# A layer norm inside a transformer decoder: two averaging matmuls against turned token rows and VectorE's statistics

## The chip, the cores and the metric

One core of a Trainium2 chip. The metric is the device time of one execution in microseconds (us). Before the change three runs gave 2074.24, 2076.47 and 2077.68 us, median 2076.47.

## The reference

A gated linear attention layer, a cross attention and a six-layer local transformer stand in a row, each with a residual and a layer norm behind it. All is float32. The change lies in the six-layer part, which takes most of the time:

```python
for i in range(6):
    x = attn_layer(shift_tokens(x), Wqkv[i], q_scale[i], k_scale[i], Wo[i]) + x
    x = ffn_layer(shift_tokens(x), ln_g[i], ln_b[i], W1[i], b1[i], W2[i], b2[i]) + x

def ffn_layer(x, g, bln, W1, b1, W2, b2):
    mu = x.mean(-1, keepdims=True)
    var = ((x - mu) ** 2).mean(-1, keepdims=True)
    xn = (x - mu) / jnp.sqrt(var + 1e-05) * g + bln
    a, gate = jnp.split(xn @ W1 + b1, 2, -1)
    return a * jax.nn.gelu(gate, approximate=False) @ W2 + b2
```

`shift_tokens` moves the upper 64 of the 128 channels one token on. The attention has 16 heads of width 64, normed and rotated queries and keys, and windows of 32 queries that see 64 keys. There are 2048 rows of 128 channels in all, handled as 4 batches of 512.

## The kernel before

The state `x_all` lies in SBUF with channels on the partitions (128 x 2048). The six layers are one long pipeline of 96 blocks of 128 tokens (`ALL_BLOCKS`), `g` = 0 to 95, and three more turns to drain it. In one turn, `step(g)`, every engine works on several blocks at once: block `g` gets its queries and keys, block `g-1` its values and scores, block `g-2` its probabilities and weighted values, block `g-3` has its heads turned. `n = g % 4` is the place in the batch. In this text *step 0, 1, 2, 3* means a turn with that `n`. The feed-forward part of the batch that is two batches back, pass `f` (24 of them), is spread over the four steps: layer norm in step 0, the first six matmuls (`hid`, a gate and a value for each of three chunks) in step 1, the second ones (`ffn_project`) in steps 1 and 2. The output projection of the batch before, `project_out`, lies in steps 2 and 3.

The order is written out by hand, one `step` function for each engine, and each engine does its instructions in that order. Engines meet through semaphores. PSUM is four pairs of banks: `bank_x` (values, then scores), `bank_y` (turned heads, turned keys, key projection, weighted values), `bank_z` (queries, turned queries, turned probabilities) and `bank_f` (feed-forward). A `turn` is eight 128 x 128 transposes by TensorE against the identity.

TensorE's step: values' projection V (L697) in two halves with one signal at its end; turn the heads (L621, 8 transposes, each half once ScalarE has the heads copied); turn the keys (8) and the queries (8, L621), for which ScalarE must have copied the turned heads out of the same bank (L997); project the keys (L617 with WK), for which the turned keys must be copied out (L1009); half of the scores (L682); turn the probabilities (L621); the other half of the scores; half of the weighting (L689); project the next queries (L617 with WQ); the other half of the weighting. Between the turn of the heads and that of the keys something of the feed-forward part or the output projection stands in every step: in step 0 `centre` (L650), a matmul with I - 1/128 that takes the channel mean off; in step 1 `hid(1)`; in step 2 one chunk of `ffn_project` (L662); in step 3 three chunks of `project_out` (L643).

The layer norm in step 0 is: VectorE's `add_projected` (L1118, L1119 into `ffn_x`, L1124 into `x_all`, at the end of the step 3 before), TensorE's `centre`, ScalarE's `square` (L947), TensorE's `variance` (L655, a matmul with 1/128 that puts the mean square on all partitions), ScalarE's `inverse` (L951 Ln, L953 Exp), VectorE's `norm` (L1131 times scale and inverse deviation, L1133 plus bias). All these work on 128 x 512 elements, and for odd `f` the three of `add_projected` come in two pieces each.

VectorE's step: multiply the queries by cosine and sine (L1101, L1106), their square sums (`sums(0)`: L1146, L1150), the same products for the keys once ScalarE has squared them (L1029), the scores' maximum and subtraction (L1182, L1186), `norm`, the keys' square sums, the row sums of the probabilities. ScalarE's step: square the queries (L977), copy the heads (L959), copy the values (L989), copy the turned heads (L997), seed the mask (L1003), copy turned keys (L1009) and queries (L1014), invert the queries' norms (L965, L969), square the keys (L1029), copy the turned probabilities (L1034), exponentials (L1041). In step 1 a table load (L983) and the first `gelu` (L941) stand before the values' copy, and VectorE's `gated(f, 0)` (L1096) releases TensorE's second `hid`, L626.

## Time and profile before

| | |
|---|---|
| median of three runs | 2076.47 us |
| the profiled execution | 2077.16 us |
| its span | 2075.4 us |
| TensorE busy | 1973.1 us, 95% of the span |
| VectorE / ScalarE / GpSimd busy | 68% / 67% / 52% |
| the pipeline of steps | about 440 to 2045 us of the span |

The profiled execution is 1.76 us longer than its span, and 0.69 us longer than the median of the runs. In the chain that ended last TensorE has 88% of the span. A busy matmul is not a matmul at its peak: in a timeline the distance from one group's start to the next group's start is what the group takes in the queue, and the duration of a single instruction is longer, since instructions overlap. The text after calls that distance a pitch.

### The profile page before, as it was taken

How to read it: one execution, taken by the hardware profiler on the slowest of the kernel's cores; microseconds unless marked ns; L12 is line 12 of the kernel's file. 1: busy time of each engine (PE TensorE's matmuls, PEld its weight loads, DVE VectorE, ACT ScalarE, POOL GpSimd, SP SyncE). 2: the span in 40 equal slices, each digit the busy share in tenths (PEclk: the TensorE clock that was granted, in tenths of full speed). 3: DMA queues.
4: the chain of work that ended last, by engine and by line, in shares of the span. 5: the costliest groups of instructions: out<-in, count | busy, mean ns of one | idle time of the engine just before them, and what ended most of it. 6: DMA issues, size and time to landing. Idle time of an engine off the chain costs nothing.

```text
span 2075.4 us, 74512 instructions
## 1 busy us (share of the span) xinstructions
PE 1973.1 (95%) x32424; PEld 1171.9 (56%) x32424; DVE 1407.7 (68%) x1975; ACT 1393.9 (67%) x2125; POOL 1086.2 (52%) x709
## 2 busy tenths in 40 slices
PE   8989897789999999999999999999999999999997
PEld 5655654355555555555555655555555555555553
DVE  1454545677777777777777777777777787777762
ACT  5565564466777667776777677767776777677763
POOL 1000000496666666666666666666666666666650
PEclk9999998799999999999999999999999999999999
DMA  3000001132223222232222323222332223222220
GB/s 118 2 1 1 2 21 31 28 77 64 63 63 94 73 73 63 64 94 73 73 63 66 92 71 78 74 60 72 85 79 73 67 63 95 73 74 63 64 63 21
DMA packets 82210, 128.37 MB, mean 62 GB/s; under 512 B 17246, under 2 KB 28124, under 8 KB 81884
## 3 DMA queue, kind: packets, MB, share of 16 engines
q1 hardware_dynamic: 81884, 123.59, 22.9%
q8 instruction: 257, 4.21, 0.9%
q14 instruction: 69, 0.57, 0.1%
HBM read 21.81 MB, written 1.05 MB: 11 GB/s over the span
## 4 chain that ended last, share of the span: by engine, by line
PE 88%; ACT 5%; DVE 4%; issue 3%; DMA 0%; ACTq 0%; SPq 0%; DVEq 0%
PE ps L621 17%; PE ps L617 16%; PE ps L643 9%; PE ps L697 9%; PE ps L682 7%; PE ps L689 7%; PE ps L427 4%; PE ps L626 3%; PE ps L662 3%; PE ps L630 3%; DVE work L1254 2%; PE ps L523 2%; PE ps L441 1%; PE ps L655 1%; PE ps L650 1%
## 5 line engine op out<-in xcount | busy, mean ns | idle before, releaser
L1424 POOL TENSOR_TENSOR work<-work,RS 128x1024 f32<-128x1024 f32 x192 | 365.2, 1902 | 386.3 <-ACT RS L969 384.6
L1101 DVE TENSOR_TENSOR work<-ps,work 128x512 f32<-128x512 f32 (+1 forms) x288 | 247.7, 860 | 328.9 <-ACT work L1029 292.3
L621 PEld LDWEIGHTS ps<-ident,work 128*128 128x128 f32 x3072 | 342.8, 141 | 141.3 <-issue 104.7
L621 PE MATMUL ps<-ident,work 128*128 128x128 f32 x3072 | 394.2, 275 | 6.3 <-ACT work L997 2.4
L1443 POOL TENSOR_TENSOR work<-work 128x1024 f32<-128x1024 f32 x96 | 225.9, 2354 | 99.0 <-DVE work L1106 99.0
L1435 POOL TENSOR_TENSOR work<-work 128x1024 f32<-128x1024 f32 x96 | 227.2, 2367 | 69.1 <-DVE work L1106 69.1
L1106 DVE TENSOR_TENSOR work<-ps,work 128x512 f32<-128x512 f32 (+1 forms) x288 | 247.2, 858 | 0.0
L1041 ACT ACTIVATE work<-work 128x1024 f32<-128x1024 f32 x96 | 101.5, 1057 | 205.1 <-DVE work L1186 204.7
L1146 DVE TENSOR_REDUCE SS<-work 128x16 f32<-128x1024 f32 x192 | 232.0, 1208 | 0.0
L689 PEld LDWEIGHTS ps<-work 64*32 64x32 f32 x12288 | 134.8, 105 | 147.7 <-issue 132.9
L617 PE MATMUL ps<-WQ,XS 128*128 128x512 f32 x384 | 189.3, 616 | 8.0 <-issue 4.4
L682 PEld LDWEIGHTS ps<-KT,work 64*32 64x32 f32 x12288 | 135.8, 105 | 105.5 <-issue 105.5
L643 PE MATMUL ps<-work,WO 128*128 128x512 f32 x384 | 193.5, 617 | 1.2 <-issue 1.2
L697 PE MATMUL ps<-WV,XS 128*128 128x512 f32 x384 | 190.9, 620 | 1.7 <-DVE work L1186 1.7
L1430 POOL TENSOR_TENSOR work<-work,RL 128x1024 f32<-128x1024 f32 x96 | 183.1, 1907 | 10.6 <-DVE RL L1197 10.6
L617 PE MATMUL ps<-WK,XS 128*128 128x512 f32 x384 | 185.0, 604 | 0.1
L682 PE MATMUL ps<-KT,work 64*32 64x64 f32 x12288 | 169.1, 224 | 15.0 <-issue 15.0
L689 PE MATMUL ps<-work 64*32 64x64 f32 x12288 | 167.6, 224 | 4.2 <-issue 3.0
L1034 ACT ACTIVATE work<-ps 128x1024 f32<-128x1024 f32 x96 | 98.3, 1024 | 85.1 <-PE ps L621 85.1
L1456 POOL TENSOR_TENSOR work<-work 128x512 f32<-128x512 f32 x16 | 16.5, 1040 | 258.5 <-PE ps L461 136.6
L989 ACT ACTIVATE work<-ps 128x1024 f32<-128x1024 f32 x96 | 98.6, 1027 | 51.1 <-PE ps L697 51.1
L1182 DVE TENSOR_REDUCE MX<-ps 128x16 f32<-128x1024 f32 x96 | 116.9, 1218 | 19.4 <-PE ps L682 19.4
(184 smaller groups left out, 3091.8 us busy)
## 6 DMA issues: line engine op xcount, KB each, us to landing
work<-work SPq DMA_DIRECT2D x576, 128.0 KB
work<-work SPq DMA_DIRECT2D x336, 64.0 KB
WQ<-in_wqkv SPq DMA_DIRECT2D x6, 512.0 KB, 3.6
WK<-in_wqkv SPq DMA_DIRECT2D x6, 512.0 KB, 4.5
WV<-in_wqkv SPq DMA_DIRECT2D x6, 512.0 KB, 3.5
WO<-in_wo SPq DMA_DIRECT2D x6, 512.0 KB, 3.8
work<-ZR SPq DMA_DIRECT2D x48, 64.0 KB
W<-in_w SPq DMA_DIRECT2D x6, 341.0 KB, 3.2
```

What stands on the lines that cost most here:

```text
L617: return mm(R[:, half, :], x_shift[:, 32 + at * 128:160 + at * 128], w[:, half * 512:half * 512 + 512], start=True, stop=True)
L621: m = nc.tensor.transpose(flat(R)[:, t * 128:t * 128 + 128], src[:, t * 128:t * 128 + 128], ident[:, :])
L643: m = mm(bank_f[:, 0, :], w_o[:, k, :], heads_t[:, k, 128 * (f % 2):128 * (f % 2) + 512], start=k == 0, stop=k == 7)
L682: m = mm(bank_x[32 * w:32 * w + 32, q, c8 * 64:c8 * 64 + 64], q_t[64 * q:64 * q + 64, c8, 32 * w:32 * w + 32], k_t[64 * q:64 * q + 64, c8, ...
L689: m = mm(bank_y[32 * w:32 * w + 32, q, c8 * 64:c8 * 64 + 64], probs_t[64 * q:64 * q + 64, c8, 32 * w:32 * w + 32], v_win[64 * q:64 * q + 6 ...
L697: m = mm(bank_x[:, q, :].rearrange('p (c d) -> p c d', d=64), x_shift[:, 32 + nb * 128:160 + nb * 128], w_v[:, :].rearrange('p (c q d) -> ...
L1101: V.tensor_tensor(h16(cos_part[:, j, cols]), h16(src), rotary_tabs[:, at:at + 64].unsqueeze(1).broadcast_to([PARTS, heads_in, 64]), ALU.mu ...
L1106: V.tensor_tensor(halves(sin_part[:, j, cols]), halves(src)[:, :, ::-1, :], rotary_tabs[:, at:at + 64].rearrange('p (s d) -> p s d', d=32) ...
L1146: V.tensor_reduce(sq_sums[:, j, :, 0], h16(squares[:, j, :]), AX, ALU.add).then_inc(done, 1)
L1424: U.tensor_tensor(h16(qk_norm[:, j, :]), h16(cos_part[:, j, :]), inv_norms[:, j, :].unsqueeze(2).broadcast_to([PARTS, 16, 64]), ALU.mult). ...
L1435: U.tensor_tensor(cos_part[:, 0, :], cos_part[:, 0, :], sin_part[:, 0, :], ALU.add).then_inc(q_rotated, 1)
L1443: U.tensor_tensor(cos_part[:, 1, :], cos_part[:, 1, :], sin_part[:, 1, :], ALU.add).then_inc(k_rotated, 1)
```

## The change

Four things are changed.

1. `centre` becomes `turn_tokens`: four transposes of `ffn_x` into `bank_f`, so that tokens lie on the partitions. It stands right behind V, ahead of the turn of the heads. `variance` becomes `turn_back`, four transposes of the normed rows, at the place of `variance`.
2. Mean and variance of a token are now taken by VectorE's row statistics (`moments`: four `bn_stats`, four `bn_aggr`), the inverse deviation by ScalarE on 128 x 4 elements instead of 128 x 512, and `norm` is four `tensor_scalar` of 128 x 128 with the mean and the inverse deviation of the row. ScalarE's `square` is gone, and `inverse` stands in its place, ahead of the queries' norms. Scale and bias are applied after the turn back by one instruction (`affine`) at the place of the old `norm`.
3. `add_projected` is cut in two. The addition into `x_all` (`add_to_x`) moves from the end of step 3 into step 0, behind the queries' sine product. `moments` follows it, then the queries' square sums, then `norm`.
4. In every step the two halves of V signal apart (`values_ready` counts twice), and ScalarE copies them in two instructions of 512 columns instead of one of 1024. Who waits for these semaphores waits for twice the count.

In the last pass, outside the steps, the same functions stand in the same order, with the last norm's instructions among them.

```diff
     ffn_x = sb('YS', [PARTS, SEQ])
-    centred = sb('YC', [PARTS, SEQ])
-    spread = sb('YQ', [PARTS, SEQ])
-    normed = sb('YR', [PARTS, SEQ])
+    centred = sb('YC', [PARTS, 4, PARTS])
+    ffn_stats = sb('YT', [PARTS, 4, 6])
+    ffn_moment = sb('YM', [PARTS, 4, 2])
+    ffn_rstd = sb('YQ', [PARTS, 4])
...
-            def centre(f):
+            def turn_tokens(f):
                 pe.wait_ge(ffn_shifted, f + 1)
                 pe.wait_ge(x_updated, f + 4)
-                mm(bank_f[:, 1, :], centre_w[:, :], ffn_x[:, :], start=True, stop=True).then_inc(ffn_centred, 1)
-
-            def variance(f):
-                pe.wait_ge(ffn_squared, f + 1)
+                for j in range(4):
+                    m = nc.tensor.transpose(bank_f[:, 1, j * 128:j * 128 + 128], ffn_x[:, j * 128:j * 128 + 128], ident[:, :])
+                m.then_inc(ffn_turned, 1)
+
+            def turn_back(f):
+                pe.wait_ge(ffn_centred, f + 1)
                 pe.wait_ge(x_plus_attn, f + 1)
-                mm(bank_f[:, 0, :], mean_w[:, :], spread[:, :], start=True, stop=True).then_inc(ffn_variance, 1)
+                for j in range(4):
+                    m = nc.tensor.transpose(bank_f[:, 0, j * 128:j * 128 + 128], centred[:, j, :], ident[:, :])
+                m.then_inc(ffn_returned, 1)
...
                     for q in range(2):
-                        m = mm(bank_x[:, q, :].rearrange('p (c d) -> p c d', d=64), x_shift[:, 32 + nb * 128:160 + nb * 128], w_v[:, :].rearrange('p (c q d) -> p q c d', q=2, d=64)[:, q], start=True, stop=True)
-                    m.then_inc(values_ready, 1)
+                        mm(bank_x[:, q, :].rearrange('p (c d) -> p c d', d=64), x_shift[:, 32 + nb * 128:160 + nb * 128], w_v[:, :].rearrange('p (c q d) -> p q c d', q=2, d=64)[:, q], start=True, stop=True).then_inc(values_ready, 1)
...
+                if f is not None and n == 0:
+                    turn_tokens(f)
                 if d:
                     pe.wait_ge(heads_copied, g - 2)
                     turn(bank_y, heads, 0, 4).then_inc(heads_turned, 1)
                     turn(bank_y, heads, 4, 8).then_inc(heads_turned, 1)
-                if f is not None and n == 0:
-                    centre(f)
...
-            def square(f):
-                act.wait_ge(ffn_centred, f + 1)
+            def inverse(f):
+                act.wait_ge(ffn_moments, f + 1)
                 if due(f):
-                    act.wait_ge(ffn_normed, f)
-                A(spread[:, :], bank_f[:, 1, :], ACT.Square).then_inc(ffn_squared, 1)
-
-            def inverse(f):
-                act.wait_ge(ffn_variance, f + 1)
-                A(spread[:, :], bank_f[:, 0, :], ACT.Ln, bias=tiny[:, 0:1]).then_inc(ffn_log, 1)
+                    act.wait_ge(ffn_centred, f)
+                A(ffn_rstd[:, :], ffn_moment[:, :, 1], ACT.Ln, bias=tiny[:, 0:1]).then_inc(ffn_log, 1)
                 act.wait_ge(ffn_log, f + 1)
-                A(spread[:, :], spread[:, :], ACT.Exp, scale=-0.5).then_inc(ffn_inverse, 1)
+                A(ffn_rstd[:, :], ffn_rstd[:, :], ACT.Exp, scale=-0.5).then_inc(ffn_inverse, 1)
...
                 if b:
-                    act.wait_ge(values_ready, g)
-                    if due(g - 1):
-                        act.wait_ge(windows_loaded, 160 * (g - 1))
-                    A(v_rows[:, (n - 1) % 2, :], flat(bank_x), ACT.Copy).then_inc(values_copied, 1)
+                    for q in range(2):
+                        act.wait_ge(values_ready, 2 * g - 1 + q)
+                        if due(g - 1):
+                            act.wait_ge(windows_loaded, 160 * (g - 1))
+                        A(v_rows[:, (n - 1) % 2, 512 * q:512 * q + 512], bank_x[:, q, :], ACT.Copy).then_inc(values_copied, 1)
...
+            def add_to_x(f):
                 dve.wait_ge(ffn_shifted, f + 1)
...
+            def moments(f):
+                dve.wait_ge(ffn_turned, f + 1)
+                if due(f):
+                    dve.wait_ge(ffn_moments, f)
+                for j in range(4):
+                    m = V.bn_stats(ffn_stats[:, j, :], bank_f[:, 1, j * 128:j * 128 + 128])
+                m.then_inc(ffn_sampled, 1)
+                dve.wait_ge(ffn_sampled, f + 1)
+                if due(f):
+                    dve.wait_ge(ffn_centred, f)
+                for j in range(4):
+                    m = V.bn_aggr(ffn_moment[:, j, :], ffn_stats[:, j, :])
+                m.then_inc(ffn_moments, 1)
+
             def norm(f):
                 dve.wait_ge(ffn_inverse, f + 1)
                 if due(f):
+                    dve.wait_ge(ffn_returned, f)
+                for j in range(4):
+                    m = V.tensor_scalar(centred[:, j, :], bank_f[:, 1, j * 128:j * 128 + 128], ffn_moment[:, j, 0:1], ffn_rstd[:, j:j + 1], ALU.subtract, ALU.mult)
+                m.then_inc(ffn_centred, 1)
+
+            def affine(f):
+                dve.wait_ge(ffn_returned, f + 1)
+                if due(f):
                     dve.wait_ge(hidden_ready, 3 * f)
-                V.scalar_tensor_tensor(out=bank_f[:, 0, :], in0=bank_f[:, 1, :], scalar=layer_vecs[:, f // 4 * 9 + 6:f // 4 * 9 + 7], in1=spread[:, :], op0=ALU.mult, op1=ALU.mult).then_inc(ffn_normed, 1)
-                dve.wait_ge(ffn_normed, f + 1)
-                V.tensor_scalar(ffn_in[:, :], bank_f[:, 0, :], layer_vecs[:, f // 4 * 9 + 7:f // 4 * 9 + 8], None, ALU.add).then_inc(ffn_input, 1)
+                V.tensor_scalar(ffn_in[:, :], bank_f[:, 0, :], layer_vecs[:, f // 4 * 9 + 6:f // 4 * 9 + 7], layer_vecs[:, f // 4 * 9 + 7:f // 4 * 9 + 8], ALU.mult, ALU.add).then_inc(ffn_input, 1)
...
+                if f is not None and n == 0:
+                    add_to_x(f)
+                    moments(f)
+                if a:
                     sums(0, g)
+                if f is not None and n == 0:
+                    norm(f)
...
                 if f is not None and n == 0:
-                    norm(f)
+                    affine(f)
```

TensorE's row at step 0 before, from V to the next V (L697 is V, L650 `centre`, L655 `variance`):

```order
647 L697 MATMUL ps<-WV,XS 128x512 x2
648 L621 MATMUL ps<-ident,work 128x128 x8
649 L650 MATMUL ps<-YS,centre_w 128x512
650 L621 MATMUL ps<-ident,work 128x128 x16
651 L617 MATMUL ps<-WK,XS 128x512 x2
652 L682 MATMUL ps<-KT,work 32x64 x32
653 L621 MATMUL ps<-ident,work 128x128 x8
654 L682 MATMUL ps<-KT,work 32x64 x32
655 L655 MATMUL ps<-YQ,mean_w 128x512
656 L689 MATMUL ps<-work 32x64 x32
```

The same place now (L704 is V, L654 `turn_tokens`, L623 the turns, L661 `turn_back`):

```order
640 L704 MATMUL ps<-WV,XS 128x512 x2
641 L654 MATMUL ps<-ident,YS 128x128 x4
642 L623 MATMUL ps<-ident,work 128x128 x24
643 L619 MATMUL ps<-WK,XS 128x512 x2
644 L689 MATMUL ps<-KT,work 32x64 x32
645 L623 MATMUL ps<-ident,work 128x128 x8
646 L689 MATMUL ps<-KT,work 32x64 x32
647 L661 MATMUL ps<-ident,YC 128x128 x4
648 L696 MATMUL ps<-work 32x64 x32
```

Nothing stands between the turn of the heads and that of the keys any more.

VectorE's row before, from the shifted addition at the end of step 3 to the first products of the keys in step 0:

```order
903 L1118 TENSOR_TENSOR YS<-ps,X 64x128
904 L1119 TENSOR_TENSOR YS<-ps,X 64x128
905 L1118 TENSOR_TENSOR YS<-ps,X 64x384
906 L1119 TENSOR_TENSOR YS<-ps,X 64x383
907 L1124 TENSOR_TENSOR X<-ps,X 128x128
908 L1124 TENSOR_TENSOR X<-ps,X 128x384
909 L1101 TENSOR_TENSOR work<-ps,work 128x1024
910 L1106 TENSOR_TENSOR work<-ps,work 128x1024
911 L1146 TENSOR_REDUCE SS<-work 128x16
912 L1150 TENSOR_REDUCE SL<-SS 128x16
913 L1101 TENSOR_TENSOR work<-ps,work 128x512
```

The same place now, for an even `f`, where the additions are in one piece (L1170 and L1174 are the square sums, L1128 the addition into `x_all`):

```order
991 L1119 TENSOR_TENSOR YS<-ps,X 64x512
992 L1120 TENSOR_TENSOR YS<-ps,X 64x511
993 L1101 TENSOR_TENSOR work<-ps,work 128x1024
994 L1106 TENSOR_TENSOR work<-ps,work 128x1024
995 L1128 TENSOR_TENSOR X<-ps,X 128x512
996 L1136 BN_STATS YT<-ps 128x6 x4
997 L1142 BN_AGGR YM<-YT 128x2 x4
998 L1170 TENSOR_REDUCE SS<-work 128x16
999 L1174 TENSOR_REDUCE SL<-SS 128x16
1000 L1150 TENSOR_SCALAR YC<-ps,YM,YQ 128x128 x4
1001 L1101 TENSOR_TENSOR work<-ps,work 128x512
```

Twelve instructions now stand between the queries' sine product and the keys' cosine product that were not there, and the addition into `x_all` has come down past the two products of the queries.

## Rows read from the trace of the kernel before

**Rows 1.** Page's chain; a stretch: us, PE, PEld, DVE, ACT, POOL busy, clock, DMA.

```profile
PE 88%; ACT 5%; DVE 4%; issue 3%; DMA 0%; ACTq 0%; SPq 0%; DVEq 0%
...
450.00:2050.00 1600.00, 1576.41 (x28774) 928.02 (x28774) 1177.49 (x1535) 1136.99 (x1782) 1009.16 (x642) 1.00 0.28 71
```

**Rows 2.** Timeline of PE, one step 0 and into step 1: start, us, line.

```profile
845.88 1.98 PE L697 MATMUL ps<-WV,XS 128*128 128x512 f32 x4
847.70 1.04 PE L621 MATMUL ps<-ident,work 128*128 128x128 f32 x8
848.57 1.02 PE L650 MATMUL ps<-YS,centre_w 128*128 128x512 f32 x2
849.56 2.05 PE L621 MATMUL ps<-ident,work 128*128 128x128 f32 x16
851.48 1.95 PE L617 MATMUL ps<-WK,XS 128*128 128x512 f32 x4
...
855.97 1.12 PE L655 MATMUL ps<-YQ,mean_w 128*128 128x512 f32 x2
857.03 0.86 PE L689 MATMUL ps<-work 64*32 64x64 f32 x64
...
865.12 1.12 PE L626 MATMUL ps<-YN,W 128*128 128x512 f32 x2
```

**Rows 3.** Timeline of ACT, the same step.

```profile
847.90 1.03 ACT L989 ACTIVATE work<-ps 128x1024 f32<-128x1024 f32 x1 [0.77 <-PE ps L697]
848.82 1.08 ACT L997 ACTIVATE work<-ps 128x512 f32<-128x512 f32 x2
...
850.72 1.10 ACT L1009 ACTIVATE KT<-ps 128x512 f32<-128x512 f32 x2
851.67 1.06 ACT L1014 ACTIVATE work<-ps 128x1024 f32<-128x1024 f32 x1
...
853.05 0.27 ACT L965 ACTIVATE LS<-SL 128x16 f32<-128x16 f32 x1
...
853.48 1.07 ACT L1029 ACTIVATE work<-ps 128x512 f32<-128x512 f32 x2
```

**Rows 4.** Timeline of DVE, the same step.

```profile
846.85 0.56 DVE L1119 TENSOR_TENSOR YS<-ps,X 64x383 f32<-64x383 f32 x1
847.45 0.76 DVE L1124 TENSOR_TENSOR X<-ps,X 128x128 f32<-128x128 f32 x2
848.12 1.22 DVE L1101 TENSOR_TENSOR work<-ps,work 128x1024 f32<-128x1024 f32 x1
...
850.38 1.21 DVE L1146 TENSOR_REDUCE SS<-work 128x16 f32<-128x1024 f32 x1
...
854.09 0.69 DVE L1101 TENSOR_TENSOR work<-ps,work 128x512 f32<-128x512 f32 x1 [2.28 <-ACT work L1029]
854.70 0.68 DVE L1106 TENSOR_TENSOR work<-ps,work 128x512 f32<-128x512 f32 x1
```

**Rows 5.** Timeline of PE, a step 2: the turns of keys and queries.

```profile
880.23 1.98 PE L697 MATMUL ps<-WV,XS 128*128 128x512 f32 x4
...
883.90 1.94 PE L621 MATMUL ps<-ident,work 128*128 128x128 f32 x16
885.83 1.95 PE L617 MATMUL ps<-WK,XS 128*128 128x512 f32 x4
```

**Rows 6.** Timeline of DVE early in the span: prices of small instructions.

```profile
52.99 1.64 DVE L1268 BATCH_NORM_STATS2 work<-work 128x6 f32<-128x128 f32 x8
...
94.62 0.80 DVE L1279 TENSOR_SCALAR work<-ps,work 128x512 f32<-128x512 f32 x1
95.34 1.11 DVE L1284 BATCH_NORM_AGGREGATE work<-work 128x2 f32<-128x24 f32 x8
```

**Rows 7.** Waits of the whole span, and PE at the last pass.

```profile
PE ps L682 <- issue: 15.0, 17, 1.5
...
2055.01 1.13 PE L626 MATMUL ps<-YN,W 128*128 128x512 f32 x2 [3.02 <-DVE YN L1133]
```

More of the change, by code:

```diff
@@ L307, in decoder @@
     gates_ready = nc.alloc_semaphore('gates_ready')
+    ffn_turned = nc.alloc_semaphore('ffn_turned')
+    ffn_sampled = nc.alloc_semaphore('ffn_sampled')
+    ffn_moments = nc.alloc_semaphore('ffn_moments')
+    ffn_returned = nc.alloc_semaphore('ffn_returned')
     HIDDEN_CHUNKS = [128, 128, 85]
@@ L361, in windows @@
                 before = v_rows[:, (m + 1) % 2, :]
-                sp.wait_ge(values_copied, m + 1)
+                sp.wait_ge(values_copied, 2 * (m + 1))
                 for q in range(2):
@@ L382, in _ @@
                         sp.dma_start(w_k[:, :], io['wqkv'][l + 1, :, 1024:2048]).then_inc(wk_loaded, 16)
-                        sp.wait_ge(values_ready, l * 16 + 16)
+                        sp.wait_ge(values_ready, 2 * (l * 16 + 16))
                         sp.dma_start(w_v[:, :], io['wqkv'][l + 1, :, 2048:3072]).then_inc(wv_loaded, 16)
@@ L752, in step @@
                 if f is not None and n == 0:
-                    variance(f)
+                    turn_back(f)
                 if f is not None and n == 1:
@@ L790, in finish @@
                 last_centre(2)
-                centre(f)
+                turn_tokens(f)
                 last_variance(2)
-                variance(f)
+                turn_back(f)
                 pe.wait_ge(ffn_input, f + 1)
@@ L1000, in step @@
                 if b:
-                    act.wait_ge(values_copied, g)
+                    act.wait_ge(values_copied, 2 * g)
                     seed = window_mask[:, 0 if n == 1 else 1, :]
@@ L1019, in step @@
                 if f is not None and n == 0:
-                    square(f)
+                    inverse(f)
                 if f is not None and n == 1:
@@ L1034, in step @@
                     A(probs_t[:, :, :], turned(bank_z), ACT.Copy).then_inc(probs_turned_copied, 1)
-                if f is not None and n == 0:
-                    inverse(f)
                 if b:
@@ L1061, in finish @@
                 last_inverse(1)
-                square(f)
                 last_square(2)
@@ L1106, in rotary_sin @@
                 V.tensor_tensor(halves(sin_part[:, j, cols]), halves(src)[:, :, ::-1, :], rotary_tabs[:, at:at + 64].rearrange('p (s d) -> p s d', d=32).unsqueeze(1).broadcast_to([PARTS, heads_in, 2, 32]), ALU.mult).then_inc(done, 1)
+            places = lambda f: ((0, 128, 384), (128, 512, 0)) if f % 2 else ((0, 512, 0),)
             def add_projected(f):
@@ L1112, in add_projected @@
                 if due(f):
-                    dve.wait_ge(ffn_centred, f)
+                    dve.wait_ge(ffn_turned, f)
                 xo = f % 4 * 512
-                parts = ((0, 128, 384), (128, 512, 0)) if f % 2 else ((0, 512, 0),)
-                for first, last, at in parts:
+                for first, last, at in places(f):
                     end = min(last, 511)
@@ L1120, in add_projected @@
                 m.then_inc(ffn_shifted, 1)
+            def add_to_x(f):
                 dve.wait_ge(ffn_shifted, f + 1)
-                for first, last, at in parts:
+                xo = f % 4 * 512
+                for first, last, at in places(f):
                     xc = x_all[:, xo + first:xo + last]
@@ L1216, in finish @@
                 add_projected(f)
+                add_to_x(f)
+                moments(f)
                 last_scale(0)
@@ L1219, in finish @@
                 norm(f)
+                affine(f)
                 last_scale(2)
@@ L1406, in stage @@
                 if due(g - 3):
-                    pool.wait_ge(values_ready, g - 3)
+                    pool.wait_ge(values_ready, 2 * (g - 3))
                 pool.wait_ge(x_updated, bt + 1)
```

3 lines of the change are left out of this document (removed).

## The prediction

> **What bounds the kernel.** I read the page's chain of waits first: TensorE (PE) has 88% of it. The table of stretches then shows it busy for 1576 of the 1600 us from 450 to 2050, at a granted clock of 1.00, its 2.4 GHz level [rows 1]. So only what shortens PE's row, or lets it wait less inside what looks busy, can help. Then I read the timelines of the three engines in one step 0 side by side, all times below counted from the start of V (845.88) [rows 2 to 4].
>
> PE: heads turned from 1.82 (the start of its row less 845.88, and so on), `centre` from 2.69, keys' and queries' turns (16) from 3.68, key projection from 5.60, `variance` from 10.09 for 1.06, weighting from 11.15. Eight transposes take 0.87 (1.82 to 2.69), so four cost 0.43. The sixteen take 1.92, against 1.74 at that pitch: PE looks busy there but is held. By what? ScalarE's row answers: values' copy at 2.02, turned heads' copies at 2.94, just as that ends, first half done some 0.60 later at 3.53, and PE goes at 3.68. Turned keys' copies begin at 4.84, the first half is done at 5.45, and the key projection starts at 5.60. Both gaps are 0.15, the usual delay from a ScalarE copy to a matmul here. So up to 5.60 step 0 is set by ScalarE, and `centre` filled a hole. Step 2 is the same to the hundredth: sixteen turns at 3.67, key projection at 5.60 [rows 5].
>
> The other thread runs from the keys' products on VectorE. They start at 8.21 (854.09), wait for ScalarE's square at 7.60, and release in turn the maximum, subtraction, exponential, two copies, two small inverses, the table load, `gelu`, `gated` and PE's second `hid` at 19.24 (865.12) [rows 2 to 4]: 11.03 later. PE by itself reaches that `hid` at the same moment: the weighting, the next queries and the weighting's second half take it from 11.15 to the next V at 14.64, then come 1.82 of V, two matmuls at 0.86, 0.2 to signal and 0.8 of `gated`, 4.6 in all: 19.24. Two threads end together, so the later one will decide.
>
> **Part by part.**
>
> *PE's matmuls.* Per pass `centre` (0.99) becomes four transposes (0.43), and `variance` (1.06 behind scores, 0.19 of it the switch from small tiles) becomes 0.43 plus a switch of about 0.15, an estimate, 0.58. Naively 1.04 x 24 = 25 us less PE work. The question is how much of it is on the path.
>
> *Values in halves.* The first half is complete 0.91 earlier. ScalarE was idle for 0.77 before the values' copy, so from 1.25 [rows 3]. It now copies half 0 until about 1.76 and half 1 from 2.02 to 2.50, at 0.48 each (two of 512 columns in 0.95, as the turned heads' copies show when the mask follows). In step 2 the first turned heads' half is ready at 2.50 too. Its copy is done at 3.10, so the keys' turns need not wait: 1.82 + 0.87 + 0.86 for the chunk of `ffn_project` = 3.55. Sixteen turns at 1.74 give 5.29. The turned keys' copy: heads' copies to 3.45, mask 0.95 to 4.40, first half done 5.01, PE may go at 5.16, so 5.29 stands. The key projection, 1.88 when late, takes 1.81 when it isn't. In sum 0.31 + 0.07, call it 0.37 a step. The keys' squares come 0.30 earlier as well, so VectorE follows. 22 passes: -8.1 us. Bounds: 0, if ScalarE is late anyway, and -0.45 a step, the whole time that it is free sooner, which is -9.9 us. In steps 1 and 3 more matmuls stand as a cover, and nothing comes of it. In the first layer's steps there is no cover at all and dependencies set the pace. I take -1 there (0 to -1.8, four times 0.45).
>
> *Step 0 up to the key projection.* `turn_tokens` takes 1.82 to 2.26 (its input is ready at 1.53 [rows 4]), heads' turn 2.26 to 3.13. ScalarE is free at 2.50 but the first turned half comes only at 2.91. Its copy ends at 3.50, PE's keys' turns at 3.65, before 3.68. ScalarE's row then runs 0.03 ahead of before and the key projection starts at 5.57. `centre`'s saving is gone: the wait takes its place, and the split pays only for that.
>
> *VectorE in step 0.* The addition moves down by two products: no change in sum, but the products come 0.7 earlier and the queries' turn, which needed the sine product, is free of it. Added: four `bn_stats`, (1.64 - 0.28) / 7 = 0.195 each; four `bn_aggr`, (1.11 - 0.20) / 7 = 0.13 each on 24 numbers, here 6, I take 0.12; four `tensor_scalar` with two scalars. That form took 0.72 pitch on 512 columns [rows 6]; less 384 columns at 1.04 ns, which the 1024 against the 512 column products show (1.13 against 0.60 [rows 4]), it is 0.32. Unpipelined each would be at most 0.28, 0.20 and 0.41. The row for an odd `f` (additions in two pieces): products from 1.56 to 3.82, addition to 4.49, `bn_stats` to 5.27, 0.1 for the result, `bn_aggr` to 5.91, queries' sums to 7.26, `norm` 1.28 to 8.54. For an even `f` the row is 0.34 earlier, but `norm` then waits for ScalarE: turned queries' copy from 5.74, 0.90, then Ln and Exp at 0.25 each, ready at 7.17, `norm` to 8.45. The keys' squares lie at 7.75 or before and are not last. So the keys' products begin at 8.54 or 8.45 in place of 8.21: 0.33 or 0.24 late. `square` held ScalarE for 0.48 (L1014 to L965 is 1.38, of which 0.90 the copy) and Ln and Exp now take as much at its place; Ln and Exp of 512 behind `variance` are gone, but there ScalarE was waiting.
>
> *The rest of step 0 and into step 1.* `turn_back` saves 0.48, but the weighting needs the keys' last product: 8.54 + 2.48 + 0.06 = 11.08, against 11.15. The second `hid` follows the products at 11.03: 19.57 or 19.48, against 19.24. `affine` (0.67) for two instructions gives VectorE 0.7 back behind the subtraction, and the keys' sums come earlier, yet ScalarE's queue behind the exponential is what the thread passes through. So a pass without a stall of PE loses 0.24 to 0.33. PE's own issue of instructions stalls in the scores now and then (17 waits, 0.9 each on average, in all kinds of steps [rows 7]). Where that comes in the second scores of a step 0, VectorE catches up, only PE's thread counts and 0.4 is saved. I read the second `hid`'s distance from V in the 22 passes one by one, 19.24 to 20.58: 8 undisturbed (19.24 to 19.30), together +2.0; 8 with PE 0.1 to 0.4 late, +0.0; 6 with PE over 0.7 late, -2.5. Sum -0.5. Bounds: with `norm` at a cost of nothing the undisturbed ones lose nothing and the late ones gain 0.25, -4.6 in all; with all twelve small instructions unpipelined (1.12 + 0.80 + 1.64 = 3.6 against 2.55), 1.0 more, +17.
>
> *Last pass.* Its norm lies open: PE waits 3.02 for the last norm row before its first `hid` [rows 7]. There 0.99 and 1.06 of matmul, the square and the Ln and Exp of 512 columns (each about 0.6, as the copies of that size) go out of a series, 3.9 in sum; 0.43 and 0.43 of transposes, 1.4 of statistics, 0.5 of Ln and Exp and 1.28 of `norm` for 0.7 come in, 3.3. With two matmul latencies less exposed to others' queues I take -1.0 (-2 to +1).
>
> Sum: -8.1 - 1 - 0.5 - 1 = -10.6 on the profiled 2077.16, 2066.6. The median of the runs is 0.69 lower; I give 2066.5.
>
> *A rule against it.* Small VectorE instructions here cost no more than their columns and about 0.06 [rows 6], but the `bn_stats` row reads SBUF, and the kernel now reads PSUM. The Trainium skill ("Perfetto Trace Analysis", Optimizing Scalar/DVE Operations) puts the access overhead of a VectorE instruction at about 60 ns for SBUF and about 125 ns for PSUM. By that the eight PSUM readers cost 0.5 more a pass, an estimate by that page, and the sum would be near 2076; rows 4 have PSUM reads of 1024 and 512 columns at 1.13 and 0.60, which leaves 0.07 for the fixed part, so I go by these. That result is my first rival.
>
> **Rivals.**
>
> 1. *VectorE's small instructions cost about 0.5 a pass more than I take.* For: no row has `bn_stats` from PSUM, nor a wait between such groups. Against: products from PSUM show a fixed part of 0.07. Price: undisturbed and late passes 16 x 0.5, nothing in the others, +8: 2075, no change.
>
> 2. *The keys' products are pushed beyond what the split gives back: slower.* Place: VectorE's row in step 0, ahead of the keys' products. It decides once they start 0.8 later than before (8.21), since then 16 x 0.8 outweighs the 10 of the other terms. At full unpipelined price it is 1.3 later, and the sum +17 - 10 = +7: 2084. For: two dependent waits, 12 short instructions. Against: rows 6 are pipelined.
>
> 3. *The split gives nothing in step 2*, since ScalarE is held by its heads' copy or a second wait costs as much: -2.5 in all, 2074. Against: it is idle 0.77 before the values' copy [rows 3].
>
> 4. *PE's stalls by issue come elsewhere or grow* when PE runs closer to its instruction fetch; 15 us in 17 waits could move by 4 either way [rows 7]. 2070 with a loss.
>
> 5. *VectorE is quick and its thread has slack.* Step 0 loses nothing: 2062; with `turn_back`'s whole 0.48 in every pass, 2055.
>
> 6. *More transposes lower the clock.* PE makes 32 transposes in every step, and the granted clock of the stretch is 1.00 [rows 1]; eight more in each fourth step should not matter. If a tenth of the 1600 us went at half the clock, 160 us would be added: 2230. The Trainium skill ("TensorE: Matmul & The Clock Gate", Part 4: PE-mode transpose) says that transposes do not count as PE being busy in the same way; the trace gives that rule no hold here.
>
> **Chances.** Forecast 0.48 (2061 to 2071); rival 1 0.15; 2 0.11; 3 and 4 0.13; 5 0.12; 6 0.01. A measurement of this kernel tells about 0.2%, 4.2 us, from no change. Faster takes the forecast, rival 5 and a part of 4 and 1: 0.69. Same 0.19, slower 0.12. The range 2058 to 2079 leaves out the lower half of rival 5 and most of 2; the likeliest case alone is 2061 to 2071.
>
> **What would show it.** Step 2 from V to the key projection 7.1 less 1.81, so 5.3 for 5.60. Step 0: key projection still at 5.57, PE or its loads held by the turned heads' copy in front of the keys' turns; weighting at 11.1; second `hid` at 19.5 where undisturbed. `bn_stats` at 0.2, `norm` four at 0.32. VectorE's keys' products waiting for nothing in odd passes. I am wrong if the key projection of step 2 still starts 5.6 behind V, or if the keys' products start beyond 8.7.

## The result, and the profile after

The changed kernel takes 2070.55 us (median of 11 runs, 2066.19 to 2074.26); the kernel before took 2077.48 in the runs beside it. The ratio is 0.9969 [0.996, 0.9977]: faster by 6.9 us. 2066.5 was predicted. The profiled execution took 2071.80 with a span of 2070.0, against 2077.16 and 2075.4: 5.4 less.

From the page: the engines' busy time, the queue that carries instructions, the shares of the chain. Then the stretch of [rows 1], with the same columns (length, busy time of PE, PEld, DVE, ACT and POOL, granted clock, DMA).

```profile
PE 1947.8 (94%) x32520; PEld 1179.6 (57%) x32520; DVE 1449.9 (70%) x2239; ACT 1371.7 (66%) x2197; POOL 1087.3 (53%) x709
...
q8 instruction: 257, 4.21, 0.9%
...
PE 73%; ACT 10%; DVE 10%; issue 6%; DMA 0%; ACTq 0%; SPq 0%; DVEq 0%
```

```profile
450.00:2050.00 1600.00, 1553.68 (x28881) 936.86 (x28878) 1222.23 (x1803) 1118.28 (x1856) 1010.84 (x642) 1.00 0.28 72
```

PE's busy time in this stretch fell by 22.7 us, just about what the prediction called naive, and its idle time rose from 23.6 to 46.3 by the same row of before [rows 1]. So PE now waits for nearly all that it saves. The chain says for whom: PE's share went from 88% to 73%, ScalarE's from 5% to 10%, VectorE's from 4% to 10%, issue from 3% to 6%. The clock stayed at 1.00.

Where the 5.4 us of the profiled executions are, measured from the start of V in one step to the start of V in the next, in us:

| part | before | after | difference |
|---|---|---|---|
| up to the first V | 396.06 | 396.91 | +0.9 |
| the first layer's seven steps | 108.04 | 107.09 | -0.95 |
| the 22 steps 0 | 330.8 | 329.2 | -1.5 |
| the 22 steps 1 | 433.5 | 436.4 | +3.0 |
| the 22 steps 2 | 364.5 | 357.9 | -6.6 |
| the 22 steps 3 | 373.5 | 373.5 | 0.0 |
| behind the last V | 69.1 | 69.0 | -0.1 |

The first line is chance: no edit touches that part, and in the other eleven traces it ends anywhere from 392.5 to 398.3.

In this text a time without a unit is in us, and a start within a step counts from the start of its V. One step 0, PE, the columns of [rows 2]; V starts at 845.52:

```profile
845.52 1.98 PE L704 MATMUL ps<-WV,XS 128*128 128x512 f32 x4
847.34 0.60 PE L654 MATMUL ps<-ident,YS 128*128 128x128 f32 x4
847.78 1.04 PE L623 MATMUL ps<-ident,work 128*128 128x128 f32 x8
849.22 1.94 PE L623 MATMUL ps<-ident,work 128*128 128x128 f32 x16 [0.40 <-ACT work L1000]
851.14 1.96 PE L619 MATMUL ps<-WK,XS 128*128 128x512 f32 x4
...
855.62 0.66 PE L661 MATMUL ps<-ident,YC 128*128 128x128 f32 x4
856.67 1.16 PE L696 MATMUL ps<-work 64*32 64x64 f32 x64 [0.39 <-DVE work L1106]
...
865.11 1.12 PE L628 MATMUL ps<-YN,W 128*128 128x512 f32 x2
```

The token rows are turned in 0.44 where `centre` took 0.99 [rows 2]. PE then stands for 0.40 in front of the keys' turns, until ScalarE's copy of the turned heads is through, and the key projection starts at 5.62; before 5.60. The way back (L661) is short too, and behind it PE waits 0.39 for a product of VectorE: the weighting starts at 11.15, as before. The second `hid` is at 19.59, before 19.24. These two waits now recur in nearly every pass. PE's waits, 450 to 2000 (us in total, times, longest), of the kernel after and then of before:

```profile
PE ps L689 <- issue: 10.6, 14, 1.3
PE ps L623 <- ACT work L1000: 10.0, 24, 0.7
PE ps L696 <- DVE work L1106: 6.9, 18, 0.4
PE ps L696 <- issue: 3.7, 8, 1.1
```

```profile
PE ps L682 <- issue: 12.6, 15, 1.5
...
PE ps L621 <- ACT work L997: 1.2, 2, 0.8
...
PE ps L689 <- DVE work L1106: 0.4, 1, 0.4
```

Two waits of 1.6 us in total became 16.9. VectorE and ScalarE in the same step 0, as in [rows 4] and [rows 3]:

```profile
850.02 0.88 DVE L1136 BATCH_NORM_STATS2 YT<-ps 128x6 f32<-128x128 f32 x4
850.93 0.38 DVE L1142 BATCH_NORM_AGGREGATE YM<-YT 128x2 f32<-128x6 f32 x4
...
852.45 0.19 DVE L1174 TENSOR_REDUCE SL<-SS 128x16 f32<-128x32 f32 x1
852.86 1.37 DVE L1150 TENSOR_SCALAR YC<-ps,YM,YQ 128x128 f32<-128x128 f32 x4 [0.22 <-ACT YQ L955]
854.14 0.68 DVE L1101 TENSOR_TENSOR work<-ps,work 128x512 f32<-128x512 f32 x1
```

```profile
846.68 0.60 ACT L992 ACTIVATE work<-ps 128x512 f32<-128x512 f32 x1
847.54 0.60 ACT L992 ACTIVATE work<-ps 128x512 f32<-128x512 f32 x1 [0.26 <-PE ps L704]
848.48 1.09 ACT L1000 ACTIVATE work<-ps 128x512 f32<-128x512 f32 x2 [0.33 <-PE ps L623]
...
851.35 1.05 ACT L1017 ACTIVATE work<-ps 128x1024 f32<-128x1024 f32 x1
852.25 0.33 ACT L953 ACTIVATE YQ<-YM,tiny 128x4 f32<-128x4 f32 x1
852.61 0.21 ACT L955 ACTIVATE YQ<-YQ 128x4 f32<-128x4 f32 x1
```

VectorE is done with the queries' sums at 7.12 and waits 0.22 for ScalarE's Exp (L955), which ends at 7.30. `norm` starts at 7.34 and the keys' products at 8.62; before 8.21. This is a pass of odd `f`, with the addition in two pieces (L1128 x2). Such a pass is called heavier below, since VectorE's row is longer in it, and one of even `f` lighter. Even in the heavier one ScalarE ends last. In 21 of the 22 passes the products start at 8.62 (8.91 in the other).

Step 2, PE, against [rows 5]: the sixteen turns take 1.75 instead of 1.93 and the key projection starts 5.30 behind V, not 5.60.

```profile
880.21 1.98 PE L704 MATMUL ps<-WV,XS 128*128 128x512 f32 x4
...
883.76 1.91 PE L623 MATMUL ps<-ident,work 128*128 128x128 f32 x16
885.51 1.02 PE L619 MATMUL ps<-WK,XS 128*128 128x512 f32 x2
```

The last pass, against [rows 7]:

```profile
2048.08 2.08 PE L628 MATMUL ps<-YN,W 128*128 128x512 f32 x2 [0.90 <-DVE YN L1157]
```

This `hid` is 6.93 earlier in the span than before, while the projection ahead of the norm (L645, before L643) ends 5.81 earlier: the open norm is shorter by 1.1. But here the first pair of matmuls took 2.08 where it took 1.13 [rows 7]. The granted clock says why. A stretch of the kernel after, then two of the kernel before, with the columns of [rows 1]:

```profile
2046.90:2053.70 6.80, 5.89 (x9) 2.52 (x8) 2.16 (x3) 1.30 (x3) 0.00 (x0) 0.50 0.11 39
```

```profile
2055.00:2056.10 1.10, 1.09 (x3) 0.62 (x4) 0.55 (x1) 0.91 (x1) 0.00 (x0) 1.00 0.07 15
2056.30:2059.60 3.30, 3.30 (x5) 1.33 (x4) 0.75 (x1) 0.79 (x2) 0.00 (x0) 0.50 0.23 82
```

After, TensorE's granted clock fell to 0.50, its 1.2 GHz level, at about 2046.9 and stayed there until 2053.7, and the first three pairs of `hid` lie in that stretch. PE had waited 1.01 and 1.71 in the norm just before. Before, it fell only at 2056.2, behind the first pair, and until 2059.6. A matmul of 512 columns has a pitch of 0.85 there instead of 0.43. The six pairs of this `hid` take 1.09 longer than before, which gives the 1.1 back.

### The profile page after: what moved, and what is told of

Its sections match the earlier page's. It is cut to its first block, busy times and chain, and to the rows that moved or that the text cites. A ratio compares the mean times of both kernels' runs of the same rounds, so it can differ in the third digit from the quotient of the medians.

```text
span 2070.0 us, 75204 instructions
## 1 busy us (share of the span) xinstructions
PE 1947.8 (94%) x32520; PEld 1179.6 (57%) x32520; DVE 1449.9 (70%) x2239; ACT 1371.7 (66%) x2197; POOL 1087.3 (53%) x709
## 4 chain that ended last, share of the span: by engine, by line
PE 73%; ACT 10%; DVE 10%; issue 6%; DMA 0%; ACTq 0%; SPq 0%; DVEq 0%
PE ps L619 13%; PE ps L623 13%; PE ps L645 9%; PE ps L704 7%; PE ps L696 6%; PE ps L689 6%; PE ps L429 4%; PE ps L669 3%; PE ps L628 3%; PE ps L632 2%; DVE work L1287 2%; DVE work L1106 2%; PE ps L525 2%; PE ps L443 1%; ACT work L1000 1%
## 5 line engine op out<-in xcount | busy, mean ns | idle before, releaser
L623 PEld LDWEIGHTS ps<-ident,work 128*128 128x128 f32 x3072 | 344.1, 141 | 118.6 <-issue 90.0
L623 PE MATMUL ps<-ident,work 128*128 128x128 f32 x3072 | 392.8, 275 | 14.6 <-ACT work L1000 11.2
L1170 DVE TENSOR_REDUCE SS<-work 128x16 f32<-128x1024 f32 x192 | 231.6, 1206 | 0.0
L645 PE MATMUL ps<-work,WO 128*128 128x512 f32 x384 | 193.4, 618 | 0.0
L704 PE MATMUL ps<-WV,XS 128*128 128x512 f32 x384 | 191.0, 620 | 1.8 <-DVE work L1216 1.8
L689 PE MATMUL ps<-KT,work 64*32 64x64 f32 x12288 | 168.6, 224 | 13.3 <-issue 13.3
L1037 ACT ACTIVATE work<-ps 128x1024 f32<-128x1024 f32 x96 | 98.5, 1026 | 84.8 <-PE ps L623 84.8
L1012 ACT ACTIVATE KT<-ps 128x512 f32<-128x512 f32 x192 | 104.1, 600 | 31.8 <-PE ps L623 31.8
```

The lines of the kernel that those rows point to most:

```text
L623: m = nc.tensor.transpose(flat(R)[:, t * 128:t * 128 + 128], src[:, t * 128:t * 128 + 128], ident[:, :])
L645: m = mm(bank_f[:, 0, :], w_o[:, k, :], heads_t[:, k, 128 * (f % 2):128 * (f % 2) + 512], start=k == 0, stop=k == 7)
L689: m = mm(bank_x[32 * w:32 * w + 32, q, c8 * 64:c8 * 64 + 64], q_t[64 * q:64 * q + 64, c8, 32 * w:32 * w + 32], k_t[64 * q:64 * q + 64, c8, ...
L704: mm(bank_x[:, q, :].rearrange('p (c d) -> p c d', d=64), x_shift[:, 32 + nb * 128:160 + nb * 128], w_v[:, :].rearrange('p (c q d) -> p q ...
L1170: V.tensor_reduce(sq_sums[:, j, :, 0], h16(squares[:, j, :]), AX, ALU.add).then_inc(done, 1)
```

## The experiments

Medians are of the runs of each kernel, ratios (with 95% intervals) against the kernel before, run beside it. Differences between two of the changed kernels are taken from their ratios, times 2077 us. Starts and sums of steps are from one profiled execution of each.

### Each half of the change alone

*Halves only*: the kernel before, with values' projection signalled and copied in halves.

```
-   m = mm(bank_x[:, q, :]...)          # two, then m.then_inc(values_ready, 1)
+   mm(bank_x[:, q, :]...).then_inc(values_ready, 1)
-   A(v_rows[:, (n - 1) % 2, :], flat(bank_x), ACT.Copy)
+   for q in range(2):
+       act.wait_ge(values_ready, 2 * g - 1 + q)
+       A(v_rows[:, (n - 1) % 2, 512 * q:512 * q + 512], bank_x[:, q, :], ACT.Copy)
```

> The kernel before with the values' projection signalled and copied in halves, the layer norm left as it was. Theory A (the copy in halves is what gains, the norm by token rows costs): the keys' projection in step 2 starts 0.37 earlier as in the changed kernel (-8), the first layer about -1, and step 0, which still has the centring matmul as a cover, gains 0.3 to 0.37 too, since ScalarE's copies and with them VectorE's products of the keys come 0.3 earlier (-7): about -16 in all, 2061, faster than the changed kernel. Rival B (the two matmuls saved on TensorE are what gains): no more than -2, about 2075. Rival C (both add up, the norm is worth nothing either way): -7, like the changed kernel, 2070.

Measured: 2060.11 us, 0.9931 [0.9917, 0.9944], near the 2061 of theory A.

*Norm only*: the changed kernel with these edits taken back.

> The changed kernel with one signal and one copy for the values, as before; the layer norm by token rows stays. Theory A: step 2 at 5.60 from the values' projection to that of the keys again, step 0 the same 5.60, VectorE's products of the keys in step 0 0.3 late, the second hidden matmul 0.2 to 0.35 late where TensorE does not stall: 0 to +5, 2077 to 2082. Rival B (less work on TensorE gains): -10 or more, 2067 or less.

Measured: 2076.93, 1.0012 [1.0002, 1.0022]: 2.5 us slower than before, and no 10 us faster as rival B had it. Its keys' products start at 8.61, its step 2 stays at 16.35. One step 0 of *halves only*, VectorE; V at 842.71:

```profile
850.85 0.69 DVE L1101 TENSOR_TENSOR work<-ps,work 128x512 f32<-128x512 f32 x1 [2.22 <-ACT work L1029]
```

The keys' products start at 8.14 there (7.88 in the lighter passes), 0.5 to 0.7 before those of the changed kernel, and the second `hid` at 19.19 (median) instead of 19.60. So the halves alone bring twice what the whole change brings, and the norm by token rows takes about half of it away: 0.0038 of 2077 is 7.9 us, of which the passes show 5.3 in the steps 0 (323.9 against 329.2), 2.2 in the steps 1, 1.1 in the steps 2.

### Where the token rows' turns stand

*Token rows behind the heads*: in the changed kernel the four transposes go behind the heads' turns.

```
-   if f is not None and n == 0: turn_tokens(f)
    (the turns of both heads)
+   if f is not None and n == 0: turn_tokens(f)
```

> The changed kernel with the four transposes of the feed-forward input behind the turn of the heads, where the centring matmul stood, and not ahead of it. Theory A (VectorE's row in step 0 sets the weighting and the second hidden matmul): the projection of the keys in step 0 starts at about 5.2 in place of 5.6, but the weighting still at 11.1 and the hidden matmul where it was: no more than -1 us against the changed kernel, about 2070. Rival D (the lost cover of the keys' turns is what holds step 0): 22 times 0.4, -9, 2062.

Measured: 2058.15, 0.9928 [0.9912, 0.9943], 8.5 less than the changed kernel by the ratios. Theory A is wrong, and rival D, the lost cover, came out. (A cover is work that PE does while ScalarE copies what PE needs next.) One step 0, PE, VectorE and ScalarE; V at 839.41:

```profile
841.23 1.04 PE L623 MATMUL ps<-ident,work 128*128 128x128 f32 x8
842.10 0.60 PE L654 MATMUL ps<-ident,YS 128*128 128x128 f32 x4
842.67 1.94 PE L623 MATMUL ps<-ident,work 128*128 128x128 f32 x16
844.59 1.96 PE L619 MATMUL ps<-WK,XS 128*128 128x512 f32 x4
...
850.23 0.86 PE L696 MATMUL ps<-work 64*32 64x64 f32 x64 [0.50 <-DVE work L1106]
```

```profile
846.33 0.18 DVE L1174 TENSOR_REDUCE SL<-SS 128x16 f32<-128x32 f32 x1
846.43 1.36 DVE L1150 TENSOR_SCALAR YC<-ps,YM,YQ 128x128 f32<-128x128 f32 x4
847.71 0.68 DVE L1101 TENSOR_TENSOR work<-ps,work 128x512 f32<-128x512 f32 x1
```

```profile
846.06 0.20 ACT L955 ACTIVATE YQ<-YQ 128x4 f32<-128x4 f32 x1
```

The four transposes now lie in the time in which ScalarE copies the turned heads, so PE's wait of 0.40 is gone and the key projection starts at 5.18. The heads are turned 0.44 earlier too, and with them ScalarE's whole row moves: its copy of the turned heads starts at 2.52 and not at 2.96, and Exp ends at 6.85. In this heavier pass `norm` then waits for nothing and starts at 7.02, as soon as VectorE is free. The products start at 8.30, the weighting at 10.82, the second `hid` at 19.27 (median). The steps 0 sum to 318.3 instead of 329.2.

*The same without the halves*, the control:

> tokens_behind_heads with one signal and one copy for the values. The turned heads' copies then start when the values' copy ends, at 2.95 as before, and the cover of 0.57 hides nothing that isn't waited for anyway: within 2 us of norm_only, about 2077. If the cover alone is worth something without the halves, 2070 or less.

Measured: 2076.7, 0.9995 [0.9983, 1.0007], with norm only at 1.0012 [1.0002, 1.0022]: 3.5 us apart with intervals that overlap. Without the halves the copy of the turned heads starts at 2.94, behind the values' copy, whatever PE does, and the key projection at 5.60: the cover is worth little or nothing. The gain of the cover needs the halves.

### Is VectorE's row the bound?

*Statistics twice*: the changed kernel computes its four `bn_stats` a second time.

```
+   for j in range(4):
+       m = V.bn_stats(ffn_stats_2[:, j, :], bank_f[:, 1, j * 128:j * 128 + 128])
```

> The changed kernel with each of the four row statistics of a pass taken a second time into a spare buffer: four more VectorE instructions of about 0.2 us, 0.78 a pass, ahead of the products of the keys. Theory A: VectorE's row is the path, so nearly every pass becomes 0.7 to 0.8 longer, less in passes where TensorE stalls late: +13 to +18 against the changed kernel, 2084 to 2088. Rival E (VectorE has slack there, ScalarE's copies set the step): +4 or less.

Measured: 2076.57, 1.0004 [0.9993, 1.0016], +7.3 against the changed kernel, between both. VectorE in one step 0; V at 845.04:

```profile
850.33 0.87 DVE L1139 BATCH_NORM_STATS2 YU<-ps 128x6 f32<-128x128 f32 x4
...
852.85 1.36 DVE L1153 TENSOR_SCALAR YC<-ps,YM,YQ 128x128 f32<-128x128 f32 x4
854.13 0.68 DVE L1102 TENSOR_TENSOR work<-ps,work 128x512 f32<-128x512 f32 x1
```

0.80 of new work moved the keys' products from 8.62 to 9.09 here, a heavier pass, and in the lighter ones to 8.69: 0.47 and 0.07 late, so VectorE had a slack of 0.3 and 0.7 under the wait for Exp. On average they are 0.27 late, and 22 x 0.27 = 5.9, most of the 7.3; the steps 0 and 1 of the profiled execution are 4.7 longer together. Neither of the two expectations (13 and more, or 4 and less) was met. So VectorE was second, close behind ScalarE, and a pass carries what is added beyond the slack.

### Taking ScalarE's wait away

*Inverse ahead*: Ln and Exp go ahead of the copy of the turned queries.

```
+   if f is not None and n == 0: inverse(f)
    (wait for the turned queries, their copy)
-   if f is not None and n == 0: inverse(f)
```

> The changed kernel with ScalarE's two small instructions for the inverse deviation ahead of its copy of the turned queries and not behind it. In the changed kernel the norm on VectorE starts at 7.33 behind the values' projection in step 0, just as ScalarE's Exp is done, though VectorE is free at 6.7 (even) or 7.0 (odd passes). Theory F (ScalarE's late inverse holds the norm, so the products of the keys, so the weighting and the second hidden matmul): products of the keys at 8.0 to 8.3 in place of 8.62, about -0.4 a pass, -8 us against the changed kernel, 2062. Rival G (VectorE's own work, or the copy of the queries that TensorE then gets 0.5 later, sets the step): within 2 us of the changed kernel or slower.

Measured: 2069.87, 0.9967 [0.9953, 0.998]: the time of the changed kernel, and not the 8 us less of theory F. The wait did go: in one heavier pass `norm` starts at 7.0 and the products at 8.3. The best step 0 is 0.44 shorter (14.19), but the median is 14.86. PE in the same pass shows what stands in the way; V at 844.46:

```profile
855.30 0.41 PE L696 MATMUL ps<-work 64*32 64x64 f32 x19
856.15 0.70 PE L696 MATMUL ps<-work 64*32 64x64 f32 x45 [0.44 <-issue]
```

The weighting starts earlier, at 10.84, and stops after 19 of its 64 matmuls. The wait is put down to "issue": nothing that the profile shows was waited for.

*Early inverse*: also the addition to `X` moves behind `affine`, the way back uses the other half of the bank, and PE waits for the sum only before its first `hid`.

```
-   pe.wait_ge(x_plus_attn, f + 1)      # was in turn_back
-   transpose(bank_f[:, 0, ...], centred[:, j, :], ident)
+   transpose(bank_f[:, 1, ...], centred[:, j, :], ident)
-   add_to_x(f)                         # ahead of the statistics
+   add_to_x(f)                         # behind affine(f)
```

> As inverse_ahead, and the addition into the residual state moved behind the affine instruction at the end of step 0's score work, with the turned back rows written to the other half of the bank pair. VectorE's row ahead of the products of the keys is 0.6 shorter. Theory F: the products of the keys then follow ScalarE's squares at about 8.2 in all passes, 0.45 earlier than in the changed kernel: -9 to -10 us against it, 2061, hardly better than inverse_ahead. If VectorE was the path after all, -14 or more.

Measured: 2071.26, 0.9969 [0.9954, 0.9984], again no gain, though the products start at 8.16 in all passes but one.

*Early inverse, token rows behind the heads*:

> early_inverse with the four transposes of the input behind the heads' turn as well. ScalarE's row is 0.44 earlier, VectorE's is short, so the products of the keys start at about 7.75, 0.87 earlier than in the changed kernel; TensorE alone would reach the weighting at the same time as their last product. Theory F with the cover restored: -17 to -19 us against the changed kernel, 2052. If the gains of the two edits do not add (another wait takes over), no better than tokens_behind_heads, 2058.

Measured: 2061.31, 0.9923 [0.9904, 0.9942], no better than with the token rows' move alone (0.9928), though its best step 0 is 13.75 (the changed kernel's 14.63) and its median one 14.01 (14.97). PE's waits of the early inverse, 450 to 2000:

```profile
PE ps L688 <- issue: 16.2, 17, 1.6
...
PE ps L695 <- issue: 6.7, 12, 1.3
```

Issue in the two groups of small matmuls (scores and weighting) has 22.9 us, in the changed kernel 14.3, before 13.3. Much of the time that was won on ScalarE and VectorE reappears as stalls of PE's issue.

### Fewer instructions on PE

If these stalls are the bound, a lighter instruction stream must let the shorter threads through. *After, light* leaves out half of the first group of scores of every step (32 of its 64 small matmuls) and puts four transposes of the identity in their place, so its output is not the reference's. Where PE does not stall, a step keeps its length: step 2 is 16.01 instead of 15.98.

```
-   scores(0, 4)
+   scores(0, 2)
+   for t in range(4): transpose(flat(bank_z)[:, t * 128:t * 128 + 128], ident, ident)
```

> The changed kernel with fewer TensorE instructions in about the same time: two of the four groups of the first scores of every step are left out (32 small matmuls with their weight loads, 0.39 us), and four transposes of the identity into a free bank stand in their place (0.43 us). 56 instructions less a step. The output is therefore not the reference's. Background: in inverse_ahead and early_inverse step 0 became 0.44 shorter where TensorE did not stall, but the stalls in the small-tile groups rose (19.5 us in the changed kernel, 20.7 and 29.7 there), and all their times were alike. Theory H (the stalls are TensorE's instruction refill, 16 KB at a time, and come where small tiles use up instructions): the stalls fall from about 20 to 10 us or less, and the time by 6 to 14 us, 2058 to 2065. Rival I (the stalls have another cause, such as the data transfers): stalls and time as in the changed kernel within 3 us.

Measured: 2056.17, 0.9917 [0.9903, 0.9932], 10.8 less than the changed kernel.

*Early inverse, light*:

> early_inverse with the same exchange of 32 small matmuls for four transposes in every step; the output is not the reference's. Theory H: with the refill out of the way the 0.44 of step 0 shows in the time, 6 to 10 us less than after_light. Rival J (what early_inverse won in step 0 was lost in waits of other engines): the same as after_light within 2 us.

Measured: 2052.36, 0.9896 [0.9881, 0.9911], -4.4 against the light changed kernel, with intervals that just overlap; its steps 0 have a median of 14.24 against 14.63, and steps 0 and 1 are 6.1 shorter together.

*Early inverse, token rows behind the heads, light*:

> early_inverse_behind with the same exchange; the output is not the reference's. Theory H: 13 to 19 us less than after_light, since step 0 is 0.9 shorter and the stalls (25.5 us in early_inverse_behind) go down as well. Rival J: 8 us less, as tokens_behind_heads against the changed kernel.

Measured: 2041.86, 0.9835 [0.9815, 0.9855], -17.0 against the light changed kernel. PE's waits of the light changed kernel, and of the light early inverse, 450 to 2000:

```profile
PE ps L623 <- ACT work L1002: 10.4, 25, 0.7
...
PE ps L696 <- DVE work L1108: 8.0, 23, 0.4
PE ps L689 <- issue: 2.0, 2, 1.3
```

```profile
PE ps L688 <- issue: 3.5, 3, 1.8
...
PE ps L695 <- issue: 2.9, 7, 0.8
```

With the stalls mostly gone, the early inverse is worth 4.4 us, where it was worth nothing with them; with the token rows' move it is 17.0, of which that move alone gave 8.5 in the full kernel. The first is less than the 6 to 10 expected. What an undisturbed pass loses shows whole here: in the light changed kernel PE waits for VectorE's `gated` in 22 passes, 8.0 us in all (2.3 in the changed kernel), and the steps 1 take 441.6 instead of 436.4. So the stalls explain a good part of why the early inverse gave nothing; that they explain all of it is not shown. Nor was the kernel before run in this light form, so what the change itself is worth without the stalls is not known.

## Why the prediction was right, and where it was wrong

The direction is right and the time 4 us too low: -10.6 predicted, -5.4 in the profile, -6.9 in the medians. (By its own 0.69 between profile and median the sum gives 2065.9, not 2066.5.)

*Step 2: right.* The pitch of every undisturbed pass fell from 16.35 to 15.98, exactly 0.37, by the two parts named. 22 of them are -8.1; -6.6 is what is left after 1.5 more in the disturbed ones. Halves only shows the term alone.

*First layer's steps: right*, -0.95 for -1. The +0.9 up to the first V is chance, as said, and so is some of the gap between forecast and profile.

*Step 0 up to the key projection: right*, 5.62 for 5.57, with the wait in front of the keys' turns. But it was taken as something to be accepted ("the wait takes its place, and the split pays only for that"). The transposes had only to stand behind the heads' turn and not ahead of it to cover it, and that is worth 8.5 us. Nor was the order followed to its end: 0.44 of ScalarE's row hangs on it.

*VectorE's prices: right.* `bn_stats` (0.88 - 0.28) / 3 = 0.20 for 0.195, `norm` (1.37 - 0.41) / 3 = 0.32 for 0.32, `bn_aggr` 0.07 for 0.12. Rival 1 fell. By the Trainium skill ("Perfetto Trace Analysis", Optimizing Scalar/DVE Operations) each PSUM reader would cost 65 ns more than an SBUF reader, an estimate from its 125 and 60 ns; the trace disagrees, `bn_stats` from PSUM has the pitch of those from SBUF [rows 6], within 5 ns.

*Steps 0 and 1, the step that failed.* "Sum -0.5" was +1.4 (-1.5 and +3.0, unrounded). Pass by pass, from V to the second `hid`, with the prediction's three groups of passes:

| passes | predicted | measured |
|---|---|---|
| 8 undisturbed | +2.0 | +3.3 |
| 8 with PE 0.1 to 0.4 late | 0.0 | +1.6 |
| 6 with PE over 0.7 late | -2.5 | -3.85 |

An undisturbed pass now has its second `hid` at 19.59 and not at 19.24, 0.35 late where 0.24 to 0.33 was predicted. The reason lies in who holds `norm`: the prediction had VectorE for odd `f` and ScalarE for even `f`, with the products at 8.54 and 8.45. It is ScalarE in both, and they start at 8.62, since the turned heads' copy starts at 2.96 for 2.91, the queries' at 5.83 for 5.74, and Ln to Exp is 0.36 for 0.25. The wait for Ln's result is not what made this dearer: the queries' pair (L967, L971) waits in the same way, and in both pairs Exp starts 0.03 behind Ln's end. Ln itself takes 0.33 here, and 0.20 to 0.27 in the queries' pair. It also reads a bias from a tile (`tiny`), which the queries' Ln does not; that this is the reason was not tried. The second group was to lose nothing, but no pass can now be earlier than 19.59, and PE's stalls came in other passes: one of this group went from 19.36 to 20.11. The third gained more than was counted, as most of its passes had no stall left and came down to 19.59. Which pass has a stall differs between two executions, so the split between the groups is in part chance; the 0.35 is not.

*Last pass: size right, sum wrong.* The norm gained 1.1 for 1.0. The sum lacked that the clock could stand at its lower level in the first `hid`, which took the 1.1 back.

*Rival 4* (issue stalls come elsewhere or grow) happened beside the forecast, small in sum: PE's waits put down to issue, 450 to 2000, went from 14.5 to 15.5, and in the weighting from 0.7 to 3.7. It got its weight as a disturbance; the experiments show such stalls as the likely next bound. *Rivals 2, 3, 5 and 6* did not happen: the products start at 8.62, below the 9.0 from which rival 2 decides; step 2 moved; step 0 has no slack; the clock is 1.00 from 450 to 2046, in which nearly all the transposes lie.

Not settled: why the early inverse draws 8 us more of stalls than the changed kernel (27.0 against 19.0 over the whole span), why Ln took longer, and the part of the light kernels' gap that stalls don't explain.

## What to carry to other kernels

When an instruction that goes away stood in a wait of another engine, look for what can stand there instead before the saving is counted; here the same four transposes were worth 8.5 us one place further on. Time both halves of a combined change: the halves of the copy alone gave -14, the norm beside it took 8 back. A price for a short instruction holds for the form from which it was read: Ln of 128x16 at 0.25 did not carry over to Ln of 128x4 with a bias, at 0.36. And before a longer time of a few instructions is put down to a stall, look at the granted clock of just that stretch; over 1600 us it reads 1.00.

## What was not expected of the hardware

PE's stalls by issue come close behind the packets that bring its instructions. The instruction queue q8 moves 257 packets of 16 KB, one each 8 us on average; in the light kernels 236:

```profile
q8 instruction: 236, 3.87, 0.8%
```

PE's 32520 matmuls and as many weight loads are 253 to a packet, and the light kernels have 5376 instructions and 21 packets less, 256 to one: so these are PE's instructions. Of the 21 stalls over 0.28 us in the small groups of the kernel before, 20 end 1.2 to 1.5 us after such a packet has landed, and the other 0.9. In the changed kernel 23 of 24 end 1.2 to 1.6 after one, in *inverse ahead* 25 of 26 within 1.1 to 1.6, in the early inverse 31 of 32 within 1.2 to 1.6. At random 6 in 100 would fall into a stretch of 0.5 us. The fetch itself takes 0.9 to 1.9.

Over the whole span the stalls of the two small groups sum to 18.0 us before, 19.0 after, 27.0 in the early inverse, and to 3.2, 6.5 and 5.5 in the three light kernels: 8% fewer packets go with most of them gone. The light kernels also have an eighth fewer small matmuls, which is where the stalls lie, so the two cannot be told apart by them. That the landing is the cause of a stall's end, and not only near it in time, was not tried.
